# Layer 0 of a two-layer transformer: half of the query-key sums moved to TensorE through strided transposes, and three steps of the pipeline reordered

## What is computed

```python
qkv = jnp.einsum('bnm,fm->bnf', x, Wqkv).reshape(b, n, 16, -1)
q, k, v = (qkv[..., :8], qkv[..., 8:16], qkv[..., 16:])
scores = jnp.einsum('bnhd,bngd->bnhg', q, k) / 8.0
out = jnp.einsum('bnhg,bngd->bnhd', jax.nn.softmax(scores, -1), v)
x = layernorm(x + out.reshape(b, n, -1) @ Wproj.T + bproj)
logits = x @ gate_w.T + gate_b            # 8 experts, top 2, softmax
x = layernorm(x + sum_e gate_e * (x @ expert_w[e] + expert_b[e]))
```

## Time and profile before

| | |
|---|---|
| median of 3 runs | 2219.46 us (2218.72 to 2219.76) |
| profiled execution | 2211.51 us, span 2209.8 us |
| busy share of the span | PE 93%, PEld 69%, DVE 81%, ACT 71%, POOL 48% |
| layer 0 | from the start to about 550 us |
| layer 1 and the experts | from about 550 us to the end |

### The profile page before, as it was taken

How to read it: one execution, slowest core, us unless ns; L and a number is a source line. 1 busy time by engine, 2 the same in 40 slices (tenths; PEclk the granted TensorE clock), 3 DMA queues, 4 the chain that set the end, 5 groups by cost and what they waited for, 6 DMA issues and landing times. The chain is left out here.

```text
span 2209.8 us, 60039 instructions
## 1 busy us (share of the span) xinstructions
PE 2053.7 (93%) x16256; PEld 1529.3 (69%) x16256; DVE 1781.4 (81%) x5918; ACT 1559.6 (71%) x3951; POOL 1060.5 (48%) x2183
## 2 busy tenths in 40 slices
PE   7999999997999999999999999999999993999990
PEld 5666666665676776777676676677677662999990
DVE  7999999993788888888888888888888884777775
ACT  3565656565788877878787887787887782777774
POOL 5777777775224334344334334433434434444444
PEclk8999999999999999999999999999999995999995
DMA  2000000000000000000000000000200001222226
GB/s 76 23 24 25 23 26 21 28 21 15 13 2 9 4 11 11 2 12 11 3 10 11 7 6 12 10 4 11 88 2 11 11 3 38 64 65 65 65 60 228
DMA packets 63634, 62.86 MB, mean 28 GB/s; under 512 B 9835, under 2 KB 58614, under 8 KB 62856
## 3 DMA queue, kind: packets, MB, share of 16 engines
q1 hardware_dynamic: 54906, 42.64, 6.4%
q0 software_dynamic: 8448, 16.93, 2.2%
HBM read 33.17 MB, written 22.69 MB: 25 GB/s over the span
## 5 line engine op out<-in xcount | busy, mean ns | idle before, releaser
L1363 DVE SCALAR_TENSOR_TENSOR restT<-ps_t,leadT 128x512 f16<-128x512 f32 (+1 forms) x768 | 459.2, 598 | 137.1 <-ACT leadT L1290 106.9
L1290 ACT ACTIVATE leadT<-ps_t 128x512 f16<-128x512 f32 (+1 forms) x768 | 403.0, 525 | 136.7 <-PE ps_t L1163 135.9
L1146 PE MATMUL ps_s<-xT_all,qm 128*128 128x512 f32 (+1 forms) x1024 | 489.9, 560 | 0.8 <-ACT qm L1271 0.8
L1163 PEld LDWEIGHTS ps_t<-ident,p 128*128 128x128 f32 x2560 | 315.3, 141 | 234.3 <-issue 169.5
L1163 PE MATMUL ps_t<-ident,p 128*128 128x128 f32 x2560 | 413.8, 276 | 8.2 <-DVE restT L1363 6.3
L1281 ACT ACTIVATE p<-ps_s,neg_max 128x512 f32<-128x512 f32 (+1 forms) x512 | 326.2, 637 | 81.1 <-DVE neg_max L1353 67.8
L1353 DVE CUSTOM_DVE_ANT_0 ps_s<-ps_s,mask 128x512 f32<-128x512 f32 (+1 forms) x512 | 320.0, 625 | 41.9 <-PE ps_s L1146 40.7
L984 POOL CAST v_parts<-v_all 128x36 bf16<-128x36 f32 x256 | 57.4, 224 | 612.6 <-PE ps_o L1177 612.3
L1146 PEld LDWEIGHTS ps_low<-xT_all,qm 128*128 128x128 f32 x1024 | 194.6, 190 | 135.6 <-issue 122.4
L1137 PE MATMUL ps_qm<-xT_all,m_all 128*128 128x512 f32 x512 | 263.9, 597 | 2.7 <-PEq L765 2.7
L274 POOL TENSOR_TENSOR pv_prod<-probs,kv 128x2048 f32<-128x2048 f32 x64 | 259.4, 4074 | 3.8 <-POOL probs L266 2.3
(11 more groups left out here) (221 smaller groups left out, 4161.9 us busy)
## 6 DMA issues: line engine op xcount, KB each, us to landing
row_in<-rows_dram SPq DMA_DIRECT2D x136, 65.0 KB
y<-results SPq DMA_DIRECT2D x16, 512.0 KB, 5.3
xT<-in_xT SPq DMA_DIRECT2D x32, 128.0 KB, 2.1
xres<-in_xT SPq DMA_DIRECT2D x32, 128.0 KB, 2.1
xT_all<-x2T SPq DMA_DIRECT2D x32, 128.0 KB, 2.0
out_x<-x SPq DMA_DIRECT2D x16, 256.0 KB, 3.4
xT_all<-in_wide SPq DMA_DIRECT2D x1, 2760.0 KB
results<-row_out,row_in POOLq DMA_INDIRECT x136
```

The source lines that it names most:

```text
L1146: mm = pe.matmul(ps_s[n], qm[j][:, n * P:(n + 1) * P], xT_all[:, bass.ds(b * S, (n + 1) * P)], start=True, stop=True)
L1163: mm = pe.transpose(ps_t[g][:, at + n * P:at + (n + 1) * P], probs[i][:, n * P:(n + 1) * P], ident[:, :])
L1290: act.activation(leadT[j][g][:, :], ps_t[g][:, 0:width[g]], ACT.Copy, scale=RAISE)\
L1363: dve.scalar_tensor_tensor(out=restT[j][g][:, :], in0=ps_t[g][:, 0:width[g]], scalar=RAISE, in1=leadT[j][g][:, :], op0=ALU.mult, op1=ALU.s ...
```

## The change

Of the two tiles of a pair, tile 0 keeps its sums on VectorE: `qk_sums` reduces half as much, and writes to SBUF (scores_0). Tile 1 is summed by TensorE: `sum_scores` takes, for each half c of the 256 scores and each d, the 128 elements of qk_prod that lie 8 apart as the stationary operand of a transposing matmul, 16 in all, accumulated in ps_scoresT. ScalarE copies that to SBUF (`copy_scoresT`), and `turn_scores` turns it back with two transposes into the second half of ps_scores. `find_max` and `shift_scores` now run once for each tile; the first waits for both.

The order changes too. On TensorE `sum_scores` comes between the two qkv products and `turn_scores` behind them, both ahead of the first `sum_heads`; `project` comes ahead of `turn_gates` and `turn_x2`. On ScalarE the exponentials move from the end of the step to behind the first two `apply_gates`, the third `apply_gates` behind `copy_gT`, and `norm2` behind `copy_oT`. On VectorE `exp_sums` and `exp_recips` come ahead of `moments_1`. On GpSimd `normalise` comes ahead of `inverse1`. The three new semaphores are scoresT_ps, scoresT_sb and scores_turned.

```diff
-        score_max = sb("score_max", [P, 2 * H])
+        scores_0, scoresT, max_1 = sb("scores_0", [P, HH]), sb("scoresT", [P, HH]), sb("max_1", [P, H])
+        ps_scoresT, scores_1 = ps_turn[:, 2 * P:4 * P], ps_scores[:, HH:2 * HH]
+
+        scores, score_max = (scores_0[:, :], scores_1), (ps_scores[:, 0:H], max_1[:, :])
...
                 def step(u, j, part):
+                    if part[2]:
+                        normalise(*before(u, j, 1))
                     if part[3]:
                         inverse1(*before(u, j, 2))
                     if part[2]:
-                        normalise(*before(u, j, 1))
                         pv_products(*before(u, j, 1), 0)
                         pv_products(*before(u, j, 1), 1)
...
+                        pe.wait_ge(scoresT_sb, min(s + 2, NP) if isinstance(s, int) else s + 2)
...
+                def sum_scores(u, j):
+
+                    s = 2 * u + j
+                    pe.wait_ge(qk_multiplied, 2 * (s + 1))
+                    when(pe, x1T_sb, s - 1)
+                    when(pe, gT_sb, s - 2)
+                    when(pe, v_sb, 2 * (s - 3))
+                    products = tile(qk_prod, 1, HH * DH).rearrange("p (c n d) -> p c n d", c=2, d=DH)
+                    for c in range(2):
+                        for d in range(DH):
+                            mm = pe.matmul(tile(ps_scoresT, c), products[:, c, :, d],
+                                           ident[:, :], start=(d == 0), stop=(d == DH - 1), is_transpose=True)
+                    mm.then_inc(scoresT_ps, 1)
+
+                def turn_scores(u, j):
+                    s = 2 * u + j
+                    pe.wait_ge(scoresT_sb, s + 1)
+                    when(pe, r2T_sb, s - 2)
+                    when(pe, scores_shifted, 2 * s)
+                    for c in range(2):
+                        mm = pe.transpose(tile(scores_1, c), tile(scoresT, c), ident[:, :])
+                    mm.then_inc(scores_turned, 1)
...
                         qkv_products(*before(u, j, -1), 0)
+                    if part[1]:
+                        sum_scores(u, j)
+                    if part[0]:
+                        qkv_products(*before(u, j, -1), 1)
+                    if part[1]:
+                        turn_scores(u, j)
                     if part[2]:
                         sum_heads(*before(u, j, 1), 0)
-                    if part[0]:
-                        qkv_products(*before(u, j, -1), 1)
                     if part[3]:
                         four_experts(*before(u, j, 2), 1, 0)
                     if part[2]:
                         sum_heads(*before(u, j, 1), 1)
                     if part[3]:
                         four_experts(*before(u, j, 2), 1, 1)
+                    if part[2]:
+                        project(*before(u, j, 1))
+                    if part[3]:
                         turn_gates(*before(u, j, 2))
                     if part[4]:
                         turn_x2(*before(u, j, 3))
-                    if part[2]:
-                        project(*before(u, j, 1))
...
-                def exponentials(u, j):
+                def copy_scoresT(u, j):
+                    s = 2 * u + j
+                    act.wait_ge(scoresT_ps, s + 1)
+                    when(act, scores_turned, s)
+                    act.copy(scoresT[:, :], ps_scoresT).then_inc(scoresT_sb, 1)
+
+                def exponentials(u, j, a):
                     s = 2 * u + j
                     when(act, probs_ready, s)
-                    for a in range(2):
-                        act.wait_ge(scores_shifted, 2 * s + a + 1)
-                        act.activation(tile(exps, a, HH), tile(shifted, a, HH), ACT.Exp, scale=0.125)\
-                           .then_inc(exps_ready, 1)
+                    act.wait_ge(scores_shifted, 2 * s + a + 1)
+                    act.activation(tile(exps, a, HH), tile(shifted, a, HH), ACT.Exp, scale=0.125)\
+                       .then_inc(exps_ready, 1)
...
                     if part[0]:
                         copy_kv(*before(u, j, -1), 0)
+                    if part[1]:
+                        copy_scoresT(u, j)
+                    if part[0]:
+                        copy_kv(*before(u, j, -1), 1)
                     if part[3]:
                         apply_gates(*before(u, j, 2), 0, 0)
                         apply_gates(*before(u, j, 2), 0, 1)
-                    if part[0]:
-                        copy_kv(*before(u, j, -1), 1)
-                    if part[3]:
-                        apply_gates(*before(u, j, 2), 1, 0)
+                    if part[1]:
+                        exponentials(u, j, 0)
+                        exponentials(u, j, 1)
+                    if part[2]:
+                        copy_oT(*before(u, j, 1))
                     if part[4]:
                         norm2(*before(u, j, 3))
-                    if part[2]:
-                        copy_oT(*before(u, j, 1))
                     if part[3]:
                         copy_gT(*before(u, j, 2))
+                        apply_gates(*before(u, j, 2), 1, 0)
                         apply_gates(*before(u, j, 2), 1, 1)
                     if part[4]:
                         copy_x2T(*before(u, j, 3))
-                    if part[1]:
-                        exponentials(u, j)
...
                 def qk_products(u, j, a):
                     s = 2 * u + j
-                    when(dve, scores_summed, s)
+                    when(dve, scoresT_ps if a else scores_summed, s)
+                    dve.sem_inc(passed, 1)
                     dve.wait_ge(kv_sb, 2 * s + a + 1)
...
                 def qk_sums(u, j):
-                    s = 2 * u + j
-                    dve.wait_ge(qk_multiplied, 2 * (s + 1))
-                    when(dve, scores_shifted, 2 * s)
-                    when(dve, r2T_sb, s - 2)
-                    dve.tensor_reduce(ps_scores[:, :], by_head(qk_prod[:, :], DH), AX_X, ALU.add)\
+
+                    s = 2 * u + j
+                    dve.wait_ge(qk_multiplied, 2 * s + 1)
+                    when(dve, scores_shifted, 2 * s - 1)
+                    dve.tensor_reduce(scores_0[:, :], by_head(tile(qk_prod, 0, HH * DH), DH), AX_X, ALU.add)\
                        .then_inc(scores_summed, 1)
 
-                def find_max(u, j):
-                    s = 2 * u + j
-                    dve.wait_ge(scores_summed, s + 1)
-                    dve.tensor_reduce(score_max[:, :], by_head(ps_scores[:, :]), AX_X, ALU.max).then_inc(max_found, 1)
-
-                def shift_scores(u, j):
-                    s = 2 * u + j
-                    dve.wait_ge(max_found, s + 1)
-                    when(dve, exps_ready, 2 * s)
-                    for a in range(2):
-                        dve.tensor_tensor(by_head(tile(shifted, a, HH)), by_head(tile(ps_scores, a, HH)),
-                                          tile(score_max, a, H).unsqueeze(2).to_broadcast([P, H, H]),
-                                          ALU.subtract).then_inc(scores_shifted, 1)
+                def find_max(u, j, a):
+                    s = 2 * u + j
+                    if a == 0:
+                        dve.wait_ge(scores_turned, s + 1)
+                        wait_alone(dve, scores_summed, s + 1, passed)
+                    when(dve, scores_shifted, 2 * (s - 1) + a + 1)
+                    dve.tensor_reduce(score_max[a], by_head(scores[a]), AX_X, ALU.max)\
+                       .then_inc(max_found, 1)
+
+                def shift_scores(u, j, a):
+                    s = 2 * u + j
+                    dve.wait_ge(max_found, 2 * s + a + 1)
+                    when(dve, exps_ready, 2 * (s - 1) + a + 1)
+                    dve.tensor_tensor(by_head(tile(shifted, a, HH)), by_head(scores[a]),
+                                      score_max[a].unsqueeze(2).to_broadcast([P, H, H]),
+                                      ALU.subtract).then_inc(scores_shifted, 1)
...
                 def step(u, j, part):
-                    if part[3]:
-                        moments_1(*before(u, j, 2))
                     if part[2]:
                         exp_sums(*before(u, j, 1))
                         exp_recips(*before(u, j, 1))
+                    if part[3]:
+                        moments_1(*before(u, j, 2))
                     if part[1]:
                         qk_products(u, j, 0)
                         qk_products(u, j, 1)
...
                     if part[1]:
                         qk_sums(u, j)
-                        find_max(u, j)
-                        shift_scores(u, j)
+                        for a in range(2):
+                            find_max(u, j, a)
+                            shift_scores(u, j, a)
```

(1 more changed line is left out.)

## The result

The changed kernel takes 2247.14 us (median of 4 runs, 2245.89 to 2248.89) against 2219.09 (2217.48 to 2219.76): a ratio of 1.0126, 95% interval 1.0114 to 1.0138. It is 28 us slower; the forecast was 2252 us, 33 slower.

The account below looks back on a forecast made before the run. TensorE's own step was taken to become the period, 16.9 us instead of 15.88. Over 29 even steps +29.6, filling +5.0 and draining -2.1 gave +32.5 on 2219.46, so 2252 us, range 2238 to 2266.

Parts of the forecast that it names:

- The old ring: Layer 0 before the change: waits from moments_1 over four engines to the next moments_1, 15.90 us, taken as the period.
- TensorE's sum: TensorE's step in layer 0: 13.94 us own issue, 2.02 for 18 added transposes, 0.5 and 0.45 of waits, 16.9 in all.
- the two waits: TensorE waiting for copies of its own results: gatesT, new, 0.45 us a step, and x1T, staying, 0.5.
- ring R: Not forecast, found by follow-up runs: second value product, moved copy_kv, gates, experts, sum_heads, projection, moments_1, inverse1, next products.
- The ring after the change: With normalise (1.23 us) and the two turns (0.43) out of the four-engine loop of waits, it takes 14.24 us.
- By these two alone a step would fall by 1.6 us: The shortened loop of waits, 14.24 us, and VectorE's lighter step, about 13.5, would cut each step by 1.6.
- The wait of `find_max`: VectorE's new wait for scores_turned: about 0.2 us a step, costing nothing where VectorE has slack.
- Filling: First steps of layer 0, until the first sum_experts at 51.21 us: +5.0 us, bounds +3 to +8.
- Draining: End of layer 0: step 32, without scores, -1.5 us, and the steps behind -0.6, by the earlier norm2.
- Strided loads: sum_scores reads every eighth element of qk_prod: no cost taken, 140 ns loads the sign; up to 57 us more, chance 0.22.
- Rival 3: Faster: the loop of waits sets the period at 14.24 us and TensorE keeps up, 47 us less, 2172; chance 0.05.
- Rival 4: TensorE's clock falls to 1.2 GHz in part of each step, total over 2350 us; chance 0.03.

Follow-up runs that it names:

- e9: Kernel before, no sums on TensorE, with normalise and exp_sums first, maxima and shifts tile by tile, exponentials behind copy_oT, project still behind the turns: ratio 1.0001, step 16.00 us.
- e4: Changed kernel with VectorE still reducing both tiles, the second tile's result unused: ratio 1.0125 to the kernel before, step 16.86 us.
- e10: Changed kernel with the second copy_kv moved back behind the first two apply_gates: ratio 1.0128 to the kernel before, step 16.85 us.
- e11: Kernel before with the reordering alone, no sums on TensorE, but the second copy_kv kept behind the first two apply_gates: ratio 1.0059, step 16.55 us.
- e5: Changed kernel with the stationary operands of sum_scores read as adjacent elements, summing wrong products: ratio 1.0119 to the kernel before, step 16.83 us.
- e8: Kernel before with 16 unused transposes of qk_prod added in step 0 between the two qkv products: ratio 0.9993, step 15.89 us.
- e1: Kernel before with the new order of all four engines, without sums on TensorE: ratio 1.0083, step 16.59 us.
- e3: Changed kernel, sums on TensorE, with the old order except the second copy_kv, which stays ahead of the first apply_gates: ratio 1.0300, step 18.19 us.
- e17: Changed kernel with the second copy_kv behind the gates and the first qkv product between turn_r2 and logits: ratio 1.0505 to the kernel before, step 19.67 us.

## Why the prediction was right, and where it wasn't

- **What bounds the kernel now: right as far as the rows go.** The old ring of 15.90 us is read from one timeline. e9 took 1.23 us out of it and most steps fell by 0.1 to 0.2 only, as VectorE, with two maxima there, stands right behind it; so no run tests the old ring by itself. The forecast for the change does not rest on it.
- **TensorE's sum: right**, 16.9 forecast, 16.85 measured; the added transposes 1.78 + 0.37 instead of 2.02, the two waits 0.47 and 0.48, forecast as 0.45 and 0.5. e4 and e10 rule out VectorE and ring R as owners of the step. And e11 is e10 with the sums off TensorE, VectorE reducing both tiles again: most steps fall from 16.85 to 16.2 or 16.3, where the next ring holds them.
- **The ring after the change: wrong.** "Ring: 14.24 us" followed the old ring with two parts cut out and did not ask which new one the moved copy closes. It is 16.6. The step that failed is taking 14.24 for the next bound, and with it "By these two alone a step would fall by 1.6 us": by itself the new order costs 0.7. The check "ScalarE starts the first gates at about 10.2, behind the added copy" came true in TensorE's longer step (315.68 - 305.47 = 10.21), but it named ScalarE's place for the gates and not the wait of the second copy ahead of them, although that wait is in the code of `copy_kv`. GpSimd's product was done at 315.31 and that copy started at 315.41, so the total held because TensorE's step is some 0.3 us longer than ring R, which the forecast had not looked at. That part is luck.
- **The wait of `find_max`**: 0.4 a step instead of 0.2, without effect, as said.
- **Filling: mis-sized in this execution.** +5.0 forecast, +1.2 measured; the same filling in e5 comes to +3.7. I added the transposes to a stretch at the lower clock and took its level as given; with them the 16 matmuls behind ran at the upper one (e8).
- **Draining: right in sign, 0.6 us short**: -2.1 forecast, -1.6 - 1.1 = -2.7 measured.
- **Strided loads: the choice was right, the row was not.** 191 ns instead of the 140 named as a sign. By the estimate from the earlier trace rows, with the 87 ns that a load of 8 columns takes now, that is (191 - 87) / 120 = 0.87 ns a column, 111 ns for 128: all of the room between two starts, 111 ns, and e5 finds 0.03 us a step. The room just sufficed; a forecast of more than that was not earned.
- **Rival 3, faster**, was put at 0.05 for TensorE's sake; with ring R at 16.6 it couldn't happen at all. **Rival 4**: the clock stayed at 1.00.

## What to carry to other kernels

Before work is moved from one busy engine to another, add up the receiving engine's own issue in one period, and its waits for copies of its own results: if that is above the period, what the giver gains is lost. A reordering removes one ring of waits and may close another; for every instruction that changes place, list what it waits for and who stands behind it, buffers and DMAs included. The effects of parts of a change do not add: here +0.7 us a step with the new order alone (e1), +2.3 with the sums and only the copy moved (e3), +1.0 with all of it.

## What the runs showed of the hardware that I had not expected

A transposing fp32 weight load of 128 columns takes 191 ns at a stride of eight elements against 141 without (e5); beside matmuls 0.11 us apart that showed as 0.03 us for sixteen.

TensorE's clock fell in this layer in kernels whose pauses are short. Mean clock from 100 to 500 us, and the longest pause that returns in each step: e17 0.92 with 1.6 to 2.1 us, e11 0.97 with 0.8 to 1.4, e9 0.97 with up to 0.9. The kernel before, with up to 0.55, held 1.00, 2.4 GHz. But the length of a pause does not decide it: e1 pauses for 1.5 to 1.8 us in each step and held 1.00 too, and so did e3 with 0.8 to 0.9. The rows of e17, e11 and e1:

```profile
100.00:500.00 400.00, 357.75 (x2109) 260.38 (x2108) 251.76 (x620) 190.22 (x676) 241.87 (x240) 0.92 0.06 20
...
100.00:500.00 400.00, 357.00 (x2127) 264.49 (x2124) 352.68 (x722) 227.66 (x796) 292.69 (x289) 0.97 0.08 24
...
100.00:500.00 400.00, 344.89 (x2119) 252.93 (x2116) 351.02 (x723) 229.35 (x795) 291.58 (x289) 1.00 0.08 24
```

What decides it is open. Where it fell, a lighter step for TensorE gave part of its gain back, in e9 1.1 to 1.2 us in every third or fourth step.
